# An audio-tower layer on one core: every engine's order within an iteration rewritten, the expert combination as three wide vector operations, and two of four rectifications moved whole to ScalarE

## The reference, cut to what matters

```python
# x: (8, 750, 64); for each of the 8 batch elements, all float32
h = conv1d(x, w_eff)                       # 16 taps, 64 -> 64 channels, 735 tokens left
n = layernorm(h)
h = h + softmax((n @ Wq.T) @ (n @ Wk.T).T / 8) @ n
n = layernorm(h)
logits = n @ gate_w + gate_b               # 16 experts, the top 2 per token, softmax of the two
e = relu(n @ w1[k] + b1[k]) @ w2[k] + b2[k]
y = n + w_top1 * e_top1 + w_top2 * e_top2
h = h + layernorm(y) * gamma + beta
```

## Time and profile before

| | |
|---|---|
| median of the two runs | 475.93 us |
| profiled execution | 475.97 us, span 474.2 us |
| TensorE matmul busy | 338.7 us (71%) |
| VectorE busy | 261.0 us (55%) |
| GpSimd busy | 197.5 us (42%) |
| ScalarE busy | 122.3 us (26%) |
| DMA engines | 32% of the time, 94 GB/s |
| mean granted TensorE clock | 0.774 of full |

### The profile page before, as it was taken

How to read it: one execution, slowest core, us unless ns; L and a number is a source line. 1 busy time by engine, 2 the same in 40 slices (tenths; PEclk the granted TensorE clock), 3 DMA queues, 4 the chain that set the end, 5 groups by cost and what they waited for, 6 DMA issues and landing times.

```text
span 474.2 us, 6924 instructions
## 1 busy us (share of the span) xinstructions
PE 338.7 (71%) x2138; PEld 218.7 (46%) x2138; DVE 261.0 (55%) x1073; ACT 122.3 (26%) x245; POOL 197.5 (42%) x241
## 2 busy tenths in 40 slices
PE   3857588587889688969896989687678675656400
PEld 1432343245646454656465646554555364544400
DVE  5258556435528675756575757756545545415305
ACT  2115215221532233224312342244114220111000
POOL 8000004600657173707370737273607472762170
PEclk9969578869699779967996799689657965566555
DMA  4950611032332234224422342324122432253110
GB/s 122 245 172 1 202 41 46 24 120 66 106 132 63 74 113 138 69 71 123 141 57 71 114 141 63 97 84 140 42 66 79 144 88 86 78 161 102 49 25 22
DMA packets 40916, 44.80 MB, mean 94 GB/s; under 512 B 11280, under 2 KB 30256, under 8 KB 40752
## 3 DMA queue, kind: packets, MB, share of 16 engines
q1 hardware_dynamic: 34736, 38.06, 26.4%
q0 software_dynamic: 6144, 6.30, 5.3%
HBM read 28.68 MB, written 15.66 MB: 93 GB/s over the span
## 4 chain that ended last, share of the span: by engine, by line
PE 45%; DVE 29%; issue 7%; POOL 7%; DMA 6%; ACT 4%; SPq 0%; POOLq 0%; DVEq 0%
PE small L960 15%; PE mix L960 12%; PE up L960 8%; PE wide L960 7%; POOL ysel L479 4%; DVE row_max L727 4%; DVE stats L672 3%; POOL x_far L468 2%; PE mix L1132 2%; DVE hidden L832 2%; DVE mean_var L675 2%; DVE cen L851 2%; DMA w_far<-wt 2%; DVE half_sum L847 2%; DVE ys L840 1%
## 5 line engine op out<-in xcount | busy, mean ns | idle before, releaser
L468 POOL DMA_INDIRECT x_far<-xn,place x96 | 94.6, 985 | 182.6 <-DVE place L818 155.8
L479 POOL DMA_INDIRECT ysel<-y_far,place x96 | 93.0, 969 | 81.3 <-DMA y_far<-ys 54.5
L960 PE MATMUL small<-xt,conv_w 128*64 128x368 f32 x256 | 51.7, 557 | 12.1 <-DVE conv_w L664 8.0
L960 PE MATMUL wide<-query,keys 64*128 64x368 f32 (+2 forms) x192 | 49.8, 623 | 3.4 <-ACT probs L539 2.3
L727 DVE TENSOR_REDUCE row_max<-wide 128x1 f32<-128x736 f32 (+1 forms) x48 | 43.0, 919 | 13.4 <-PE wide L960 13.4
L539 ACT ACTIVATE probs<-wide 128x736 f32<-128x736 f32 (+2 forms) x48 | 37.5, 783 | 36.1 <-PE wide L960 35.6
L1132 PE MATMUL mix<-ident,xs 128*128 128x128 f32 x112 | 25.4, 359 | 28.2 <-DMA xs<-x_far 15.1
L960 PE MATMUL mix<-wt,hidden 128*128 128x64 f32 x256 | 38.1, 312 | 1.9 <-ACT xs_t L494 1.0
L960 PE MATMUL small<-probs,xn 128*64 128x368 f32 (+2 forms) x192 | 38.5, 500 | 0.0
L960 PEld LDWEIGHTS mix<-wt,hidden 128*128 128x128 f32 x256 | 36.0, 225 | 3.8 <-issue 2.8
L960 PEld LDWEIGHTS small<-xt,conv_w 128*64 128x64 f32 x256 | 20.2, 159 | 35.7 <-issue 21.7
(11 more groups left out here) (149 smaller groups left out, 447.3 us busy)
## 6 DMA issues: line engine op xcount, KB each, us to landing
more<-w_far SPq DMA_DIRECT2D x88, 128.0 KB, 2.2
xs<-x_far SPq DMA_DIRECT2D x24, 256.0 KB, 2.8
y_far<-ys SPq DMA_DIRECT2D x24, 256.0 KB, 2.0
xt<-x_t SPq DMA_DIRECT2D x8, 375.0 KB, 3.5
w_far<-wt SPq DMA_DIRECT2D x1, 2048.0 KB, 7.5
x_far<-xs SPq DMA_DIRECT2D x2, 864.0 KB, 6.8
wt<-w SPq DMA_DIRECT2D x3, 512.0 KB, 8.1
x_far<-xn,place POOLq DMA_INDIRECT x96
```

Source lines behind the costliest of these rows:

```text
L468: pool.indirect_dma_start(x_far[r % 2], bass.IndirectOffsetOnAxis(ap=place[r % RING][:, k:k + 1], axis=0), xn2[r % RING][:, 1, k % NT, :], ...
L479: pool.indirect_dma_start(ysel[:, k // NT, k % NT, :], None, y_far[m % 2], bass.IndirectOffsetOnAxis(ap=place[m % RING][:, k:k + 1], axis= ...
L960: return pe.matmul(dst, lhsT, rhs, start=start, stop=stop, skip_group_check=True)
```

## The change

`combine` becomes three wide operations, and the moments and the sum with beta leave it for a function of their own, `prepare`:

```diff
-                for t in range(NT):
-                    dve.scalar_tensor_tensor(half_sum[:, t, :], ysel[:, 0, t, :], gates[n % RING][:, 0, t:t + 1],
-                                             xn2[n % RING][:, 0, t, :], ALU.mult, ALU.add).then_inc(s_comb, 1)
-                dve.wait_ge(s_comb, NT * (n + 1))
-                for t in range(NT):
-                    dve.scalar_tensor_tensor(cen2[:, t, :], ysel[:, 1, t, :], gates[n % RING][:, 1, t:t + 1],
-                                             half_sum[:, t, :], ALU.mult, ALU.add).then_inc(s_sum2, 1)
-                dve.wait_ge(s_sum2, NT * (n + 1))
+                dve.tensor_tensor(weighed[:], ysel[:], gates[n % RING][:].unsqueeze(3).broadcast_to([P, 2, NT, D]),
+                                  ALU.mult).then_inc(s_comb, 1)
+                dve.wait_ge(s_comb, 2 * n + 1)
+                dve.tensor_tensor(half_sum[:], weighed[:, 0], weighed[:, 1], ALU.add).then_inc(s_comb, 1)
+                dve.wait_ge(s_comb, 2 * n + 2)
+                dve.tensor_tensor(cen2[:], half_sum[:], xn2[n % RING][:, 0], ALU.add).then_inc(s_sum2, 1)
+                dve.wait_ge(s_sum2, n + 1)
+
+            def prepare(n):
+
                 moments(2, n, cen2)
```

`rectify_even` becomes `rectify`: for groups 0 and 1 ScalarE does both halves in one 128x1024 operation, for groups 2 and 3 the halves stay divided. TensorE's waits are put into one helper:

```diff
-                act.activation(hidden[:, q % 2, 0, 0:w], up[:, 0, 0:w], ACT.Relu).then_inc(s_ha, 1)
+                n = 2 if g < 2 else 1
+                act.activation(hidden[:, q % 2, 0:n, 0:w], up[:, 0:n, 0:w], ACT.Relu).then_inc(s_ha, 1)
...
+            def rectified(q):
+
+                pe.wait_ge(s_ha, q + 1)
+                if q % GROUPS >= 2:
+                    pe.wait_ge(s_hb, 2 * (q // GROUPS) + q % GROUPS - 1)
```

More of the change, by code:

```diff
@@ L382, in program @@
                     store_y(m2, 3)
+                if live(m1):
+                    for g in range(GROUPS):
+                        load_slots(m1, g)
                 if live(i - 3):
@@ L385, in program @@
                 if live(m1):
-                    for g in range(GROUPS):
-                        load_slots(m1, g)
-                    load_weights(m1, 3, 7)
+                    load_weights(m1, 4, 8)
                     store_y(m1, 0)
-                    load_weights(m1, 7, MORE)
+                    load_weights(m1, 8, MORE)
                     store_y(m1, 1)
@@ L908, in program @@
                 if live(m2):
+                    rectify_odd(m2, 2)
+                if live(n3):
+                    prepare(n3)
+                if live(m2):
                     y_copy(m2, 2)
                     rectify_odd(m2, 3)
-                if live(n3):
-                    finish(n3)
+                if live(f):
+                    keys_round(f)
                 if live(m2):
                     y_copy(m2, 3)
-                if live(f):
-                    keys_round(f)
                 if live(b):
@@ L924, in program @@
                     reduce_max(f, 0)
-                    reduce_max(f, 1)
                 if live(b):
                     normalise_again(b)
-                if live(m1):
-                    rectify_odd(m1, 0)
                 if live(f):
+                    reduce_max(f, 1)
                     reduce_max(f, 2)
-                    reduce_max(f, 3)
+                if live(n3):
+                    finish(n3)
                 if live(b):
                     route(b)
+                if live(f):
+                    reduce_max(f, 3)
                 if live(m1):
@@ L1201, in program @@
                 if live(m2):
+                    first_layer(m2, 2)
+                if live(b):
+                    scores(b, 3)
+                    weigh_values(b, 0)
+                    weigh_values(b, 1)
+                if live(m2):
                     slots_to_features(m2, 3)
                 if live(b):
-                    scores(b, 3)
+                    scores(b, 4)
+                    weigh_values(b, 2)
                 if live(m2):
@@ L1226, in program @@
                     project(f)
+                if live(m2):
+                    second_layer(m2, 3)
                 if live(b):
@@ L1234, in program @@
                 if live(c):
-                    convolve(c, 0, 4)
+                    convolve(c, 2, 3)
+                if live(m1):
+                    slots_to_features(m1, 1)
+                if live(c):
+                    convolve(c, 3, 4)
                 if live(m1):
@@ L1264, in program @@
                     rank_picks(b)
+                if live(m1):
+                    second_layer(m1, 1)
+                if live(b):
                     count_ends(b)
```

94 lines of the change are left out of this document (39 added, 55 removed).

## The result

The changed kernel takes **451.81 us** (450.88 and 452.74), against 475.93 before: 0.949 of it, with a 95% interval of 0.939 to 0.959. The forecast was 456. The profiled execution has a span of 449.1 us against 474.2, and a mean granted clock of 0.795 against 0.774.

A forecast was written before the change was run, and what follows sets the result against it. TensorE's list was taken as nearest bound, with a transfer loop beside it. Head 77.4, element 1 44.3, stretches 3 to 6 172.0, stretch 7 44.5, stretch 8 43.3, tail 72.1: span 453.6, forecast 456 us, range 444 to 473.

The forecast's parts named there:

- the stretch of 42 to 44 us: Sign of a correct forecast: middle stretches from `place` to `place` take 42 to 44 us; 43.0 was booked for each.
- The waits of a full iteration: TensorE's idle time in a full iteration, listed wait by wait, 5.0 us in sum, against 7.6 before.
- The clock term: Low clock per full iteration costs 2.0 us instead of 3.5: 1.7 on `second_layer(m1, 1)`, 0.3 on small matmuls, scores at full level.
- its loop: Transfer loop, `place` through scatter and load to next `place`: 20.65 us to slots plus 21.3 to 21.7, 42.0 to 42.3.
- rival A: Clock stays up through the counting, `second_layer` gives 1.7 back: 40.7 us in six stretches, 444 in all; chance 0.10.
- Rivals B and D: B: half the gain, 466 to 473 us, chance 0.25. D: waits move without shrinking, tail alone gains, 470 to 476, 0.08.
- The wide rectification: One ScalarE operation of 1.02 us against 0.60 per half; by the rows, undoing wins at most 0.4 at each place.
- The 0.64 struck before `second_layer(m2, 2)`: TensorE's 0.64 us wait goes, as moments and beta sum no longer stand ahead of `rectify_odd(m2, 2)` on VectorE.
- Combination: VectorE's twelve operations become three wide ones, 2.52 to 2.15 us; VectorE is no bound inside an iteration.
- The head's +1.5: Head grows by 1.5 us to 77.4: `gate_logits` comes two chunks later, `reduce_max` 3 stands behind `route`.
- Stretch 8 and the tail: Stretch 8: 43.3 us, from 43.0. Tail: 72.1, from 75.2, its two gathers starting earlier, 2.7 in all by the second.
- Rival C: Slower: waits in the second half, clock falls at `query_round` without recovering before the seam; 52 us stretches, 492 in all; chance 0.07.

The follow-up runs named there:

- seam_back: Changed kernel with `slots_to_features(m2, 2)` put back ahead of `scores` 0 and 1; 462.92 us, 0.973 of the kernel before.
- second_layer_back: Changed kernel with `second_layer(m1, 1)` put back between `count_picks` and `sum_picks`; 459.79 us, 0.964 of the kernel before.
- filler_query: query_first_conv3 plus filler's unread matmuls, without the 6 ahead of `max_scores` 0; 420.98 us, 0.876 of the kernel before.
- query_first: Changed kernel with `query_round(f)` ahead of `y_copy(m2, 3)` and `scale_attention(b)` on VectorE; 457.59 us, 0.958 of the kernel before.
- wide_only: Kernel before the change with only the three wide combination operations and the gather's wait, all orders as before; 478.76 us, 0.998 of the kernel before.
- split_relu: Changed kernel with groups 0 and 1 rectified in halves on both engines, VectorE's behind `reduce_max` 1 and 4; 458.95 us, 0.962 of the kernel before.
- prepare_first: Changed kernel with the moments and the sum with beta directly behind `combine`, ahead of `centre(f)`; 449.76 us, 0.939 of the kernel before.
- tail_order: Changed kernel; without convolution, first layer ahead of group 1's transposes, `rectify` before ScalarE's copy; elements 5 to 7 rectified in halves; 446.93 us, 0.935.
- query_first_conv3: query_first with a third convolution chunk ahead of the slots; 452.02 us, 0.943 of the kernel before.
- filler: Changed kernel with 444 more matmuls, identity products that nobody reads, placed in TensorE's waits; 423.35 us, 0.879 of the kernel before.

## Why the prediction held, and where it did not

**Direction and size** held: 456 forecast, 451.8 measured. In part this is luck: of the span's terms, the head, element 1 and stretches 3 to 7 came out 11.4 us below the forecast, and stretch 8 and the tail 6.9 above it. Of the signs that the prediction named, the 0.6 for `shift`, the 1.3 on ScalarE, the full clock behind the seam and the missing waits came; the stretch of 42 to 44 us (41.0) and the `second_layer` near 3.6 (1.98) did not.

**The waits of a full iteration** came almost as listed: 0.72 for `shift` (0.65), 0.15 before `project` (0.2; the view names no releaser), 1.42 for `query_round` (1.5), 0.28 before `to_features_again` (0.3), 1.22 before `count_picks` (1.3), 0.64 before `rank_picks` (0.64), none before `count_ends` (0). Idle was 4.6 us where 5.0 stood. seam_back and second_layer_back show that two of the removed waits were truly removed by the steps named.

**The clock term was placed wrongly**, and this is the larger part of the 2.0 us between 43.0 and 41.0; 0.7 of them is the margin that the prediction added to its loop. From the slots to `place` it had 21.3 to 21.7 us; measured are 19.7 (223.26 to 243.0), behind 21.3 up to the slots, where it had 20.65. The prediction put the low level on `second_layer` of group 1, 1.7 us, inside the loop that sets the stretch. That layer ran at full clock, which is rival A's mechanism. What holds the clock up there is not shown; with the layer back at its old place the clock falls behind the counting again. The low spell lies behind `query_round` instead (1.16 us on two chunks, 0.46 on the transposes, from 2.62 - 1.46 and 1.12 - 0.66), where the full iteration still has to take it. Part of that is hidden under the transfer: slots that come 20.2 us behind the scatter at 202.34 (filler_query's number) would have kept TensorE until 222.54 anyway, so of 1.62 us some 1.2 count, an estimate. A's 40.7 is what the steady stretches measured, to 0.3, and its chance of 0.10 was too small. The argument against it, that every iteration falls today behind that gap, rested on the gap alone: query_first has the same gap of 1.22 with the fall, the changed kernel without it. A's 444 for the whole was missed, through stretch 8 and the tail. Rivals B and D lie above the measured interval, and wide_only, seam_back and second_layer_back show against D that the orders do the work.

**The wide rectification was undervalued.** The step said that the engines are equal by the row, so undoing it could win at most 0.4 at each place. Undoing it costs some 7 us in all. The rows gave the duration of the operation rightly (1.02 forecast and measured); the price was the place of the other half in VectorE's list, behind a `reduce_max` of 0.92, and the clock behind the longer wait. The Trainium skill ("ScalarE: Activation LUTs", Rules for kernel authors) says to use VectorE for relu, up to about three times faster per element in bf16; the prediction's estimate from it was 0.2 us for a VectorE half and 1.6 us gained per iteration. The half took 0.68 us here, in float32, and split_relu is slower; bf16, or the whole rectification on VectorE, no run here shows.

**The 0.64 struck before `second_layer(m2, 2)`** did go, but not for the reason given. TensorE's timeline of the kernel before:

```profile
269.16 1.97 PE L960 MATMUL mix<-more,hidden 128*128 128x64 f32 x16 [0.64 <-ACT xs_t L494]
```

The wait ended with ScalarE's copy of group 3 (`slots_copy`, done at 269.02), not with `rectify_odd(m2, 2)`, which VectorE had done by 267.53. In the new order a `scores` and a `weigh_values` stand between the transposes of group 3 and this layer and cover the copy. In prepare_first the moments are back ahead of `rectify_odd(m2, 2)`, and there is still no wait before this layer; the 1.55 stands before `scores(b, 4)`, for an `exponential`, and the stretch is as long. So moving the moments bought nothing that shows here.

**Combination** 2.52 to 2.15: the wide operation takes 0.95 and the two others 0.56 each (the list of groups, for the wide one):

```profile
L846 DVE TENSOR_TENSOR weighed<-ysel,gates 128x768 f32<-128x768 f32 x8 | 7.6, 952 | 16.3 <-DMA ysel<-y_far,place 16.3
```

The size was right, and "no bound inside an iteration" also: wide_only shows no effect.

**The head's +1.5** does not show in the total: the first scatter starts at 76.75, against 76.72 in the earlier trace rows. Two thirds of it did come. From the end of the convolution's first four chunks (64.36; 65.28 before) to `count_ends` (73.62; 73.59 before) it takes 9.3 us instead of 8.3, with a new wait before `count_picks`:

```profile
70.32 0.28 PE L962 MATMUL up<-consts,pick 128*96 128x128 bf16 x2 [0.83 <-DVE pick L765]
```

In this execution those four chunks ended 0.9 sooner, which hides it. In second_layer_back and prepare_first, whose heads are the same, it did not, and the first scatter starts at 78.07 and 78.19.

**Stretch 8 and the tail** were the two terms with the wrong sign: 45.4 for 43.3, and 76.9 for 72.1. TensorE's timeline of the tail:

```profile
391.79 1.12 PE L1138 MATMUL mix<-ident,xs 128*128 128x128 f32 x4 [6.94 <-DMA xs<-x_far]
393.69 1.08 PE L1138 MATMUL mix<-ident,xs 128*128 128x128 f32 x4 [0.78 <-ACT xs_t L496]
394.70 2.08 PE L962 MATMUL up<-xs_t,wt 64*128 64x128 f32 x16
397.90 3.67 PE L962 MATMUL mix<-wt,hidden 128*128 128x64 f32 x16 [1.12 <-ACT hidden L574]
401.50 2.08 PE L962 MATMUL up<-xs_t,wt 64*128 64x128 f32 x16
404.71 3.67 PE L962 MATMUL mix<-wt,hidden 128*128 128x64 f32 x16 [1.12 <-ACT hidden L574]
```

From the slots at 391.79 to the `y_copy` of group 1 it takes 16.6 us; before it took 11.6, with both `second_layer` at 1.97. Two other runs divide the 5.0 us. prepare_first has the same orders here and the higher clock:

```profile
400.89 2.00 PE L961 MATMUL mix<-wt,hidden 128*128 128x64 f32 x16 [1.12 <-ACT hidden L574]
```

There it takes 12.4 us, and the tail 72.6 at 0.55. wide_only has the old orders and the low clock (3.64 and 3.65 for the two layers): 15.9 us, and the tail 77.2 at 0.50. So the clock is 4.2 of the 5.0, and the new order and the undivided rectification together are 0.7 or 0.8, which tail_order gives back. From there to the second gather 2.9 us are saved (14.9 for 17.8); the forecast had 2.7 in all. The spine of the gathers was read rightly; the step that failed in the tail is that its clock was taken as unchanged. With it unchanged, in prepare_first, the tail is 72.6, where 72.1 stood; and it falls to 0.50 with the old orders too, so the loss in the tail is not shown to come from the change. For stretch 8 the fall from 0.74 to 0.65 was booked at nothing as well, and tail_order shows that the new order has a part in it.

**Rival C's rule** (in the Trainium skill, "TensorE: Matmul & The Clock Gate", HAM oscillation: a recurring wait can make each step start at the low clock) holds in half: the fall does recur at the same place of each iteration (0.96 three times), but it costs 1.2 to 1.6 us, not 9. The page tells of waits for transfers of some 3 to 5 us in each step; the one here is 1.42 us, so C went beyond the page's case.

**Still open:** what decides whether a given wait is followed by a fall. The same 1.42 is followed by one in the changed kernel and not in prepare_first, the same 1.22 not there and in query_first. Nor does a fall stand right behind a wait: in the earlier trace rows a whole `second_layer` runs at full clock between them. Nor were the new orders of SyncE and GpSimd's gather tried alone.

## What to carry to other kernels

In this kernel, and perhaps in others where TensorE's list is the bound and has waits of about a microsecond scattered in it: price each wait with the clock that may follow it, and expect that removing one wait can lose, and adding one can cost nothing. Before such orders are tuned further, try to fill the waits with matmuls that nobody reads: it gave 28 us here, more than the whole reordering, and afterwards orders can be compared by their waits again. Where a stretch or a tail came out longer, compare it with a run at the same clock before blaming the order. Moving work to another engine costs its place in that engine's list, and here that was more than its duration; and an order made for the full iterations has to be looked at again where the work that covered it runs out.

## What the runs showed of the hardware

- The iterations lock. Three stretches of the changed kernel are 40.96, 40.96 and 40.95 us, each with the fall at the same place; prepare_first repeats 40.96, 40.97 and 40.96 at full clock throughout. In query_first_conv3 no two neighbours are equal.
- A filler is cheap at the full clock: ahead of `scores` 0 three products take 0.83 us, and the scores behind them start without the 0.72 for `shift` (TensorE's timeline of filler):

```profile
274.85 0.83 PE L962 MATMUL wide<-ident 128*128 128x128 f32 x6
275.73 1.51 PE L962 MATMUL wide<-query,keys 64*128 64x368 f32 x8
```

- In the filler kernel's full iterations (matmuls busy 38.45 of 39.30 us in the stretch shown) the clock is 1.00 throughout; it is 1.00 throughout prepare_first's steady stretches as well. In the changed kernel's tail it is 0.50 from the first microsecond to the last.
- The same tail comes at two clocks: 76.9 us at 0.50 in the changed kernel and 72.6 at 0.55 in prepare_first; with the old orders 77.2 at 0.50 in wide_only and 75.2 at 0.55 in the kernel before.
